# AdaLN block on one core: another order of the first superblock (silu, LayerNorm in pieces, q's first product, h's low part on VectorE)

## Chip, cores, metric

One core of a Trainium2 chip. The metric is the device time of one launch in microseconds. Time before: median 930.48 us of 3 runs (928.63 to 931.09).

Engines are named as the profile names them: PE is TensorE's matmul, PEld its weight load, DVE is VectorE, ACT ScalarE, POOL GpSimd, SP SyncE. PSUM has 8 banks of 512 fp32 per partition.

## What is computed

x has 4096 tokens of 256 features. Six vectors come from a small modulation product; the block is a gated attention with softmax over features and tokens (linear attention), and a mixture of 8 experts, 2 per token.

```python
mod = (silu(c) @ wmod).reshape(6, 256)          # sa, ca, ga, sb, cb, gb
ga, gb = (2 * (g >= 0) - 1) * maximum(abs(g), 0.25)
h = layernorm(x) * (1 + ca) + sa
q, k, v = split(h @ w_qkv)                      # 16 heads of 64
q = softmax(q * 64**-0.5, axis=-1)              # over the 64 features of a head
k = softmax(k, axis=-2)                         # over the 4096 tokens
context = einsum('bhnd,bhne->bhde', q, k)
out = einsum('bhde,bhnd->bhne', context, v)
x = x + ga * (merge(out) @ w_out + b_out)
h = layernorm(x) * (1 + cb) + sb
x = x + gb * moe(h)                             # top 2 of 8 experts, gelu, 1024 hidden
```

## The kernel before

The program is written engine by engine, each engine's instructions in a fixed order by hand; engines wait for each other on counting semaphores (`s_...`), and `after(eng, s, n)` is such a wait for n > 0. There is no planner: what stands behind a waiting instruction on its engine waits too.

**Tiling.** The 32 tiles of 128 tokens form 8 superblocks (SBN) of 4 tiles (ST). The k loop has 64 steps n = (superblock s, head pair j), 8 per superblock. The products with w_qkv are made exact by splitting both sides: w into `wqk_hi` (a rounded copy by ScalarE) and `wqk_lo` (the rest, `w_low` on DVE), h into `h_q[..., 0]` (high part, ScalarE, `h_hi`) and `h_q[..., 1]` (low part, GpSimd, `h_lo`, from the full h in `h_all`). A product is three terms per 128 features: 6 matmuls of 512 columns.

**Stages of a superblock.** DVE makes LayerNorm's statistics (`layer_norm`, lines 834 to 847: one bn_stats per tile, one bn_aggr per tile, then 12 small linked operations for the inverse root, each waiting for the one before). ScalarE normalises (`norm_x`, L632), PE transposes x (`x_T`, L1209), ScalarE and GpSimd make h_hi, h_all and h_lo (L620, L622, L498). Then PE makes q per tile (`q_mm`, L1227, both halves of 512 columns), DVE subtracts the maximum (`q_a`, L856 and L857), ScalarE takes the exponential (`q_e`, L638), DVE sums (`q_b`, L863 and L864), and GpSimd normalises (`q_norm`, L504).

**A step of the k loop** on PE: the k product of head pair j (`k_mm`, L1266), the four transposes of the k of the step before (`k_T`, L1275), the context product of three steps before (`c_mm`, L1285), in j = 3 the x transposes of superblock s + 2, and one half of a q product of superblock s + 1 (L1227). On DVE (lines 926 to 948): `acc` adds a finished context product (L924), `k_m` the running maximum (L916, L917), then q_a in even steps or q_b in odd ones; after step 7 `layer_norm((4, 5, 6, 7))`, after step 15 the gates (L943 to L948). On ScalarE: `k_e` (the exponential of k, L649, and the rescaling factor, L651), `k_ev` (L643), `norm_x` in j = 0 and 1, `h_hi` in j = 3, `q_e` in even steps.

**What stands before the loop.** SP issues the loads in this order (L407 to L422): c, b1, x of superblock 0, wmod's first third, w_q, w_k, x of superblock 1, the rest of wmod, four small ones, x of superblocks 2 to 7, w_out. DVE: `layer_norm((0,))`, silu, memset of ctx_acc, w_low(0), the first modulation's copies, w_low(1 to 3), the second modulation's copies, `layer_norm((1,))`, q_a(0, 0), q_a(0, 1), the gating weights (L899 to L903), q_b and q_a of the other tiles, `layer_norm((2, 3))`, q_b(0, 3). PE: first modulation (L1198), x_T(0), second modulation and gate rows (L1198, L1240), q_mm(0, 0), q_mm(0, 1), x_T(1), gating products (L1250, L1254), q_mm(0, 2), q_mm(0, 3), loop. ScalarE: silu's exponential, norm_x(0), w's high parts for q (L659), h_hi(0), those for k (L665), norm_x(1), q_e(0, 0), q_e(0, 1), h_hi(1), q_e(0, 2), q_e(0, 3), loop. `LN_OF` says which LayerNorm call a superblock waits for.

After the loop the context is folded with w_out and w_v, the residual, the second LayerNorm and the routing are done, and the experts run in hardware loops; that part (from about 350 us on) is not touched.

Of the kernel before, what the change touches and what calls it, by code (L numbers as in the profile page):

```python
# [82 lines left out]
def adaln_block(nc, x, w_qkv, w_out, b_out, Wg, bg, W1, b1, W2, b2, cvec, wmod, out):  # L83
    ctx = ExitStack()
    with ctx:
# [176 lines left out]
        s_hhi = sem("s_hhi")  # L262
        s_hlo = sem("s_hlo")
        s_kt = sem("s_kt")
        s_nm = sem("s_nm")
# [74 lines left out]
        DMA2 = 32  # L340
        CONSTS = 7
        IOTAS = 5


        KT, TR, CX = 4, 6, 7
        LN_OF = (0, 1, 2, 2, 3, 3, 3, 3)
        KN = SBN * J
# [10 lines left out]
        def xt_bank(s, c):  # L358

            return (TR, CX)[c] if s == 1 else c  # L360

# [39 lines left out]
        def _(sp):  # L401
# [10 lines left out]
            wqk_t = w_qkv[:, 0:2 * HD].rearrange("(c p) n -> p c n", p=P)  # L412
            sp.dma_start(wqk_raw[:, :, 0:HD], wqk_t[:, :, 0:HD]).then_inc(s_wq, 16)
            sp.dma_start(wqk_raw[:, :, HD:2 * HD], wqk_t[:, :, HD:2 * HD]).then_inc(s_wk, 16)
            sp.dma_start(x_all[:, ST:2 * ST, :], x_t[:, ST:2 * ST, :]).then_inc(s_x[1], 16)
            sp.dma_start(wmod_sb[:, :, 2 * D:6 * D], wmod_t[:, :, 2 * D:6 * D]).then_inc(s_wmod[1], 16)
            sp.dma_start(bo_bc[:, :], b_out.partition_broadcast(P)).then_inc(s_small, 16)
            sp.dma_start(bg_bc[:, :], bg.partition_broadcast(P)).then_inc(s_small, 16)
            sp.dma_start(wg_raw[:, :, :], Wg.rearrange("(c p) e -> p c e", p=P)).then_inc(s_small, 16)
            for s in range(2, SBN):  # L420
                sp.dma_start(x_all[:, s * ST:(s + 1) * ST, :], x_t[:, s * ST:(s + 1) * ST, :]).then_inc(s_x[s], 16)
# [56 lines left out]
        def _(pool):  # L478
# [14 lines left out]
                      allow_small_or_imprecise_dtypes=True).then_inc(s_const, 1)  # L493

            def h_lo(s, c):

                pool.wait_ge(s_hhi, s * C + (c + 1))
                pool.tensor_tensor(h_q[:, s % HB, 1, c, :], h_all[:, c, s * STOK:(s + 1) * STOK], h_q[:, s % HB, 0, c, :].bitcast(F32), ALU.subtract).then_inc(s_hlo, 1)  # L498
# [17 lines left out]
            for s in range(-1, SBN - 1):  # L516
                if s == -1:
                    for c in range(C):
                        h_lo(0, c)
                q_norm(s + 1, 0)  # L520
                if s + 2 < SBN:
                    for c in range(C):
                        h_lo(s + 2, c)
                for i in range(1, ST):
                    q_norm(s + 1, i)
                if s >= 1:
                    add_bias(s - 1)
# [82 lines left out]
        def _(act):  # L610
            act.sem_inc(s_gelu, FOUR)

            def h_hi(s, c):

                act.wait_ge(s_xt, s * C + (c + 1))
                if c == 0 and s >= HB:
                    act.wait_ge(s_kt, (s - HB + 1) * J)
                    act.wait_ge(s_hlo, (s - HB + 1) * C)
                bank = xt_bank(s, c)
                act.activation(h_q[:, s % HB, 0, c, :], ps[:, bank, :], ACT.Identity, bias=modc[:, 0, c:c + 1],  # L620
                               scale=modc[:, 1, c:c + 1])
                act.activation(h_all[:, c, s * STOK:(s + 1) * STOK], ps[:, bank, :], ACT.Identity, bias=modc[:, 0, c:c + 1],  # L622
                               scale=modc[:, 1, c:c + 1]).then_inc(s_hhi, 1)
# [30 lines left out]
            act.wait_ge(s_cTc, 1)  # L654
            act.activation(silu_t[:, :], silu_c[:, :], ACT.Exp, scale=-1.0).then_inc(s_silu_e, 1)
            norm_x(0)
            act.wait_ge(s_wq, 16)
            for c in range(C):
                act.activation(wqk_hi[:, c, 0:HD], wqk_raw[:, c, 0:HD], ACT.Copy).then_inc(s_whqk, 1)  # L659
            act.wait_ge(s_modr, 1)  # L660
            for c in range(C):
                h_hi(0, c)
            act.wait_ge(s_wk, 16)
            for c in range(C):
                act.activation(wqk_hi[:, c, HD:2 * HD], wqk_raw[:, c, HD:2 * HD], ACT.Copy).then_inc(s_whqk, 1)  # L665
            norm_x(1)
            q_e(0, 0)
            q_e(0, 1)
            for c in range(C):
                h_hi(1, c)  # L670
            q_e(0, 2)
            q_e(0, 3)

            for n in range(KN):
# [10 lines left out]
                if j % 2 == 0:  # L685
                    if j and s + 1 < SBN:
                        q_e(s + 1, j // 2 - 1)
                    elif not j and s:
                        q_e(s, ST - 1)
# [128 lines left out]
        def _(dve):  # L818
# [14 lines left out]

            def layer_norm(sbs):

                r = slice(sbs[0] * ST, (sbs[-1] + 1) * ST)
                for s in sbs:
                    dve.wait_ge(s_x[s], 16)
                    for t in range(s * ST, (s + 1) * ST):
                        last = dve.bn_stats(ln_s[:, t, :], x_all[:, t, :])  # L840
                link(last)
                for t in range(r.start, r.stop):
# [23 lines left out]
            def w_low(n):  # L866

                dve.wait_ge(s_whqk, n + 1)
                col = slice((n // C) * HD, (n // C + 1) * HD)
                dve.tensor_tensor(wqk_lo[:, n % C, col], wqk_raw[:, n % C, col], wqk_hi[:, n % C, col].bitcast(F32), ALU.subtract).then_inc(s_wlqk, 1)  # L870

            layer_norm((0,))
            dve.wait_ge(s_cT, 1)
# [6 lines left out]
            dve.tensor_copy(silu_b[:, :, :], bc(silu_c[:, :], 2, [P, C, P])).then_inc(s_silu, 1)  # L880
            dve.memset(ctx_acc[:, :, :], 0.0)
            link(dve.memset(k_new[:, 1, :], BIG))
            w_low(0)
            dve.wait_ge(s_mod, 1)
            link(dve.tensor_copy(modc[:, 0:2, :].rearrange("p k c -> p (k c)"), ps[:, MA, 0:2 * C]))
            dve.tensor_scalar(modc[:, 1, :], modc[:, 1, :], 1.0, None, ALU.add).then_inc(s_modr, 1)
            w_low(1)
            w_low(2)
            w_low(3)
            dve.wait_ge(s_mod, 2)  # L890
            link(dve.tensor_copy(modc[:, 2:4, :].rearrange("p k c -> p (k c)"), ps[:, MB, 0:2 * C]))
            link(dve.tensor_scalar(modc[:, 3, :], modc[:, 3, :], 1.0, None, ALU.add))
            dve.tensor_copy(shift_b[:, :, :], bc(modc[:, 2, :], 2, [P, C, P]))
            dve.tensor_copy(gate_raw[:, :, :].rearrange("p k d -> p (k d)"), ps[:, MG, :]).then_inc(s_modr, 1)
            layer_norm((1,))
            q_a(0, 0)
            q_a(0, 1)
            dve.wait_ge(s_small, 48)
            dve.tensor_tensor(wg_mod[:, :, :], wg_raw[:, :, :], bc(modc[:, 3, :], 2, [P, C, E]), ALU.mult).then_inc(s_wgm, 1)  # L899
            dve.wait_ge(s_bgp, 1)  # L900
            dve.tensor_tensor(bg_bc[:, :], bg_bc[:, :], ps[:, MB, 0:E], ALU.add)
            dve.wait_ge(s_wgm, 1)
            dve.tensor_tensor(wg_mod[:, :, :], wg_mod[:, :, :], bc(ps[:, MB, E:2 * E], 1, [P, C, E]), ALU.subtract).then_inc(s_bgr, 1)  # L903
            q_b(0, 0)
            q_a(0, 2)
            q_b(0, 1)
            q_a(0, 3)
            q_b(0, 2)
            layer_norm((2, 3))
            q_b(0, 3)  # L910

# [14 lines left out]
            for n in range(KN):  # L926
                s, j = divmod(n, J)
                for m in products(n - 1):
                    acc(m)
                k_m(n)  # L930
                s_, i = (s + 1, j // 2 - 1) if j >= 2 else (s, ST - 1)
                if 0 < s_ < SBN:
                    if j % 2:
                        q_b(s_, i)
                    else:
                        q_a(s_, i)
                if s == SBN - 1 and j == 1:
                    dve.wait_ge(s_xt, SBN * C)
                    dve.memset(ctx_n[:, :, :], 0.0).then_inc(s_zero, 1)
                if s == 0 and j == 7:  # L940
                    layer_norm((4, 5, 6, 7))
                if s == 1 and j == 7:
# [240 lines left out]
        def _(pe):  # L1183
# [28 lines left out]
            def q_mm(s, i, halves=(0, 1)):  # L1212

                n = s * ST + i
                if 0 in halves:
                    if i == 0:
                        pe.wait_ge(s_hlo, s * C + C)
                    if i == 2 and 1 <= s < SBN - 1:
                        pe.wait_ge(s_hhi, (s + 2) * C)
                    after(pe, s_qs, n - 1)  # L1220
# [13 lines left out]
            pe.wait_ge(s_cTc, 1)  # L1234
            x_T(0)
            pe.wait_ge(s_wmod[1], 16)
            modulation(MB, (3, 4))
# [4 lines left out]
            last.then_inc(s_mod, 1)  # L1242
            pe.wait_ge(s_wlqk, 2)
            q_mm(0, 0)
            q_mm(0, 1)
            pe.wait_ge(s_modr, 2)
            x_T(1)
            pe.wait_ge(s_small, 48)
# [6 lines left out]
            last.then_inc(s_bgp, 1)  # L1255
            q_mm(0, 2)
            q_mm(0, 3)
            pe.wait_ge(s_wlqk, 4)
            pe.wait_ge(s_bgr, 1)
# [210 lines left out]
```

## Time and profile before

| | us |
|---|---|
| median of 3 runs | 930.48 |
| profiled execution | 930.57 |
| its span | 928.8 |
| PE busy | 827.7 (89%) |
| DVE busy | 569.8 (61%) |
| ACT busy | 498.5 (54%) |
| POOL busy | 335.7 (36%) |
| mean granted TensorE clock | 0.949 of full |

The span runs from the first to the last recorded instruction; the execution's own time has 1.7 us around it. Busy shares are means over stages with different limits. In the page's picture of 40 slices (23 us each), PE's digits begin with 5 8 4 9 7: the two low ones (slices 0 and 2) are the start and the entry to the k loop. Matmul ends are modelled, and consecutive matmuls overlap in the records: six of 512 columns take 1.39 us of the chain though each row shows 0.39.

### The profile page before, as it was taken

Reading aid. Unit: us, or ns where it says so; the run is one execution under the profiler, and the core shown is the slowest. Engines: PE = TensorE matmul, PEld = TensorE weight load, DVE = VectorE, ACT = ScalarE, POOL = GpSimd, SP = SyncE. Lnnn points to the kernel's source line nnn. Section 1 sums busy time; section 2 is a strip of 40 time slices with the busy share of each in tenths; the row PEclk is TensorE's granted clock in tenths of the full one; section 3 lists DMA queues with packets and bytes.
Section 4 is the critical chain, followed back from the end, with each engine's and each line's share of the span. In section 5 each row is a group of like instructions: output and inputs, shape, how many; then the busy total and the mean of one; then the engine's idle time right before and its main releaser. Section 6 shows DMA issues by size and latency. Waiting matters only on the chain.

```text
span 928.8 us, 17546 instructions
## 1 busy us (share of the span) xinstructions
PE 827.7 (89%) x5836; PEld 771.0 (83%) x5837; DVE 569.8 (61%) x1257; ACT 498.5 (54%) x978; POOL 335.7 (36%) x304
## 2 busy tenths in 40 slices
PE   5849789999999879985499999999999999999994
PEld 4638678888888767974399999899999999999994
DVE  4667787777777642579455644656546565665552
ACT  4325446456554341369475755657566565755552
POOL 1223133333332230300124545445445554444442
PEclk9879899999999998995599999999999999999998
DMA  8300000000000003234534252424325252222222
GB/s 292 100 0 1 1 1 1 1 1 1 1 1 1 25 25 122 92 128 136 160 71 91 46 134 44 130 46 112 58 46 136 46 130 42 45 46 45 41 47 28
DMA packets 45212, 57.50 MB, mean 62 GB/s; under 512 B 7794, under 2 KB 39220, under 8 KB 45044
## 3 DMA queue, kind: packets, MB, share of 16 engines
q0 software_dynamic: 14400, 20.24, 13.7%
q1 hardware_dynamic: 30772, 36.76, 11.8%
q8 instruction: 21, 0.34, 0.2%
q14 instruction: 19, 0.16, 0.1%
HBM read 38.24 MB, written 18.75 MB: 61 GB/s over the span
## 4 chain that ended last, share of the span: by engine, by line
PE 72%; DVE 14%; issue 6%; ACT 4%; DMA 2%; POOL 1%; DVEq 0%; SPq 0%; ACTq 0%; POOLq 0%
PE ps L1433 22%; PE ps L1421 18%; PE ps L1266 7%; PE ps L1227 7%; PE ps L1285 5%; PE ps L1335 3%; PE ps L1404 2%; PE ps L1275 2%; DVE q_max L856 2%; ACT at_lo L736 2%; DVE w_lo L1170 2%; DMA wmod_sb<-in_L_wmod 1%; DVE k_blk L916 1%; PE ps L1355 1%; DVE w_lo L1167 1%
## 5 line engine op out<-in xcount | busy, mean ns | idle before, releaser
L791 ACT ACTIVATE hid<-ps,b_col 128x256 f32<-128x256 f32 x296 | 122.3, 464 | 114.4 <-PE ps L1421 98.5
L1433 PE MATMUL ps<-w_hi,hid_hi 128*128 128x256 f32 x592 | 170.9, 289 | 10.0 <-DVE hid_lo L1150 10.0
L1150 DVE TENSOR_TENSOR hid_lo<-hid,hid_hi 128x512 fp32r<-128x512 f32 x148 | 100.6, 691 | 119.5 <-ACT hid_hi L799 118.6
L1421 PE MATMUL ps<-xT_hi,w_hi 128*128 128x256 f32 x592 | 168.5, 285 | 2.2 <-DVE xT_lo L1127 2.2
L1421 PE MATMUL ps<-xT_hi,w_lo 128*128 128x256 f32 x592 | 168.2, 284 | 0.0
L1421 PE MATMUL ps<-xT_lo,w_hi 128*128 128x256 f32 x592 | 168.1, 284 | 0.0
L1433 PE MATMUL ps<-w_hi,hid_lo 128*128 128x256 f32 x592 | 166.5, 281 | 0.0
L1433 PE MATMUL ps<-w_lo,hid_hi 128*128 128x256 f32 x592 | 166.4, 281 | 0.0
L580 POOL DMA_INDIRECT out<-y,y_id x74 | 126.5, 1709 | 51.8 <-DVE y L1159 34.6
L504 POOL TENSOR_TENSOR q_n<-q_exp,q_rec 128x1024 f32<-128x1024 f32 x32 | 61.0, 1906 | 214.1 <-DVE q_rec L864 214.1
L1433 PEld LDWEIGHTS ps<-w_hi,hid_hi 128*128 128x128 f32 x592 | 111.5, 188 | 12.2 <-DVE hid_lo L1150 12.2
L1421 PEld LDWEIGHTS ps<-xT_hi,w_hi 128*128 128x128 f32 x592 | 113.7, 192 | 2.6 <-issue 2.6
L1421 PEld LDWEIGHTS ps<-xT_lo,w_hi 128*128 128x128 f32 x592 | 113.8, 192 | 0.0
L1421 PEld LDWEIGHTS ps<-xT_hi,w_lo 128*128 128x128 f32 x592 | 113.7, 192 | 0.0
L1433 PEld LDWEIGHTS ps<-w_lo,hid_hi 128*128 128x128 f32 x592 | 111.9, 189 | 0.0
L1433 PEld LDWEIGHTS ps<-w_hi,hid_lo 128*128 128x128 f32 x592 | 111.4, 188 | 0.0
L649 ACT ACTIVATE k_exp<-ps,k_new 128x512 f32<-128x512 f32 x64 | 44.0, 687 | 122.8 <-DVE k_new L917 122.8
L799 ACT ACTIVATE hid_hi<-hid 128x512 fp32r<-128x512 f32 x148 | 93.5, 632 | 10.9 <-issue 5.2
L1227 PE MATMUL ps<-wqk_hi,h_q 128*128 128x512 f32 x256 | 97.9, 427 | 0.0
L568 POOL DMA_INDIRECT listed<-xrows,gid x76 | 80.5, 1059 | 43.6 <-POOL gid L564 32.1
L916 DVE TENSOR_REDUCE k_blk<-ps 128x1 f32<-128x512 f32 x64 | 44.1, 689 | 68.5 <-PE ps L1266 68.5
L1285 PE MATMUL ps<-q_n,k_tok 128*128 128x128 f32 x512 | 70.1, 281 | 17.4 <-DVE ctx_acc L924 16.9
(194 smaller groups left out, 1511.2 us busy)
## 6 DMA issues: line engine op xcount, KB each, us to landing
w_raw<-in_L_ffn_W SPq DMA_DIRECT2D x16, 1024.0 KB
x_all<-in_L_attn_x SPq DMA_DIRECT2D x8, 512.0 KB, 10.6
out<-x_all SPq DMA_DIRECT2D x8, 512.0 KB, 3.0
xrows<-x_all SPq DMA_DIRECT2D x8, 512.0 KB, 3.0
wqk_raw<-in_L_attn_w_qkv SPq DMA_DIRECT2D x2, 1024.0 KB, 8.8
listed<-xrows,gid POOLq DMA_INDIRECT x76
out<-y,y_id POOLq DMA_INDIRECT x74
wmod_sb<-in_L_wmod SPq DMA_DIRECT2D x1, 1024.0 KB, 12.9
```

Source lines behind the costliest of these rows:

```text
L504: pool.tensor_tensor(q_n[:, s % 2, i, :].rearrange("p (h d) -> p h d", d=DH), q_exp[:, i % 2, :].rearrange("p (h d) -> p h d", d=DH), bc(q ...
L568: pool.indirect_dma_start(listed[:, i, :], None, xrows[:, :], bass.IndirectOffsetOnAxis(ap=gid[:, i:i + 1], axis=0)).then_inc(s_rows, 16)
L580: pool.indirect_dma_start(out[:, :], bass.IndirectOffsetOnAxis(ap=y_id[:, i:i + 1], axis=0), y[:, i, :], None, compute_op=ALU.add).then_in ...
L791: ins = act.activation(hid[:, m, :], ps[:, k, (m % 2) * BT:(m % 2 + 1) * BT], ACT.Gelu_apprx_tanh, bias=b1_col[:, bass.ds(e, 1), m])
L799: act.activation(hid_hi[:, m, :], hid[:, m, :], ACT.Copy).then_inc(s_hidhi, 1)
L916: link(dve.tensor_reduce(k_blk[:, j:j + 1], ps[:, KT + n % 2, :], AX, ALU.max, negate=True))
L1150: dve.tensor_tensor(hid_lo[:, m, :], hid[:, m, :], hid_hi[:, m, :].bitcast(F32), ALU.subtract).then_inc(s_hid, 1)
L1227: last = pe.matmul(ps[:, b + half, :], a, w, start=st, stop=sp_)
L1266: last = pe.matmul(ps[:, KT + n % 2, :], w, a, start=st, stop=sp_)
L1285: last = pe.matmul(ps[:, CX, 0:P], k_tok[:, n % KR, t, :], q_n[:, s % 2, t, j * P:(j + 1) * P], start=t == 0, stop=t == ST - 1)
L1421: last = pe.matmul(ps[:, k, (m % 2) * BT:(m % 2 + 1) * BT], w, a, start=st, stop=sp_)
L1433: last = pe.matmul(ps[:, Y0 + i, 0:D], a, w, start=m == 0 and st, stop=m == M - 1 and sp_)
```

## The change

- **Start.** silu's operations come ahead of LayerNorm 0 on DVE; the memset of ctx_acc moves to GpSimd. `layer_norm` is split into `ln_stats(tiles)` and `ln_finish(superblocks)`.
- **Transfers.** x of superblocks 1 and 2 is loaded ahead of w_k.
- **h of superblock 0.** ScalarE makes only the high part; DVE makes the full h and the low part itself (`h_0`), GpSimd's h_lo(0) goes. The transposed x of superblock 0 lies in banks 2 and 3.
- **w of q.** It is split in halves of 512 columns on ScalarE (`w_high`) and DVE (`w_low(0..3)`); w_k keeps its two full ones (`w_low(4)`, `w_low(5)`).
- **q's first product** is written out: the terms with h's high part first for each half, those with the low part last. It and q_mm(0, 1) come ahead of the second modulation.
- **Second modulation** is read later by DVE, behind LayerNorm 1 and 2, q_a(0, 1), q_b(0, 0), w_low(4) and w_low(5); the gate rows are copied by ScalarE (semaphore `s_modg`), which x_T(1) waits for.
- **q's last tile.** q_b(0, 2), q_a(0, 3), q_b(0, 3) and q_e(0, 3) move into steps 0 and 1 of the loop.
- **LayerNorm.** Superblocks 1 and 2 together before the loop; statistics of 3 tiles in each of steps 1, 3, 5 (8 tiles in all), the finish of superblocks 3 and 4 in step 7; statistics of 2 tiles in each odd step from 9 to 19, the finish of 5 to 7 in step 21.

The diff without its context lines, with 8 columns of indentation cut and the two new semaphores left out:

```diff
-CONSTS = 7
+CONSTS = 8
...
-LN_OF = (0, 1, 2, 2, 3, 3, 3, 3)
+LN_OF = (0, 1, 1, 2, 2, 3, 3, 3)
...
-    return (TR, CX)[c] if s == 1 else c
+    return (TR, CX)[c] if s == 1 else 2 + c if s == 0 else c
...
+    for s in (1, 2):
+        sp.dma_start(x_all[:, s * ST:(s + 1) * ST, :], x_t[:, s * ST:(s + 1) * ST, :]).then_inc(s_x[s], 16)
...
-    sp.dma_start(x_all[:, ST:2 * ST, :], x_t[:, ST:2 * ST, :]).then_inc(s_x[1], 16)
...
-    for s in range(2, SBN):
+    for s in range(3, SBN):
...
+    pool.memset(ctx_acc[:, :, :], 0.0).then_inc(s_const, 1)
...
-        if s == -1:
-            for c in range(C):
-                h_lo(0, c)
...
-            act.wait_ge(s_hlo, (s - HB + 1) * C)
+            after(act, s_hlo, (s - HB) * C)
...
-        act.activation(h_q[:, s % HB, 0, c, :], ps[:, bank, :], ACT.Identity, bias=modc[:, 0, c:c + 1],
-                       scale=modc[:, 1, c:c + 1])
+        hi = act.activation(h_q[:, s % HB, 0, c, :], ps[:, bank, :], ACT.Identity, bias=modc[:, 0, c:c + 1],
+                            scale=modc[:, 1, c:c + 1])
+        if s == 0:
+            hi.then_inc(s_hhi, 1)
+            return
...
+    def w_high(half, c):
+        col = slice(half * 512, (half + 1) * 512)
+        act.activation(wqk_hi[:, c, col], wqk_raw[:, c, col], ACT.Copy).then_inc(s_whqk, 1)
...
-    for c in range(C):
-        act.activation(wqk_hi[:, c, 0:HD], wqk_raw[:, c, 0:HD], ACT.Copy).then_inc(s_whqk, 1)
+    w_high(0, 0)
+    w_high(0, 1)
...
+    w_high(1, 0)
+    w_high(1, 1)
...
+    q_e(0, 0)
...
-    q_e(0, 0)
...
+    act.wait_ge(s_mod, 2)
+    act.activation(gate_raw[:, :, :].rearrange("p k d -> p (k d)"), ps[:, MG, :], ACT.Copy).then_inc(s_modg, 1)
...
-    q_e(0, 3)
...
-            elif not j and s:
+            elif not j:
...
-    def layer_norm(sbs):
+    def ln_stats(tiles):
+        for t in tiles:
+            if t % ST == 0:
+                dve.wait_ge(s_x[t // ST], 16)
+            last = dve.bn_stats(ln_s[:, t, :], x_all[:, t, :])
+        return last
+    def ln_finish(sbs):
...
-        for s in sbs:
-            dve.wait_ge(s_x[s], 16)
-            for t in range(s * ST, (s + 1) * ST):
-                last = dve.bn_stats(ln_s[:, t, :], x_all[:, t, :])
-        link(last)
...
-        col = slice((n // C) * HD, (n // C + 1) * HD)
+        col = slice((n // C) * 512, (n // C + 1) * 512) if n < 2 * C else slice(HD, 2 * HD)
...
-    layer_norm((0,))
+    def h_0(c):
+        dve.wait_ge(s_hhi, c + 1)
+        link(dve.tensor_scalar(h_all[:, c, 0:STOK], ps[:, xt_bank(0, c), :], modc[:, 1, c:c + 1], modc[:, 0, c:c + 1], ALU.mult, ALU.add))
+        dve.tensor_tensor(h_q[:, 0, 1, c, :], h_all[:, c, 0:STOK], h_q[:, 0, 0, c, :].bitcast(F32), ALU.subtract).then_inc(s_hlo0, 1)
...
-    dve.memset(ctx_acc[:, :, :], 0.0)
+    link(ln_stats(range(ST)))
+    ln_finish((0,))
...
+    w_low(1)
...
-    w_low(1)
+    dve.wait_ge(s_modr, 1)
+    h_0(0)
+    h_0(1)
...
+    q_a(0, 0)
+    link(ln_stats(range(ST, 3 * ST)))
+    ln_finish((1, 2))
+    q_a(0, 1)
+    q_b(0, 0)
+    w_low(4)
+    w_low(5)
...
-    dve.tensor_copy(shift_b[:, :, :], bc(modc[:, 2, :], 2, [P, C, P]))
-    dve.tensor_copy(gate_raw[:, :, :].rearrange("p k d -> p (k d)"), ps[:, MG, :]).then_inc(s_modr, 1)
-    layer_norm((1,))
-    q_a(0, 0)
-    q_a(0, 1)
+    dve.tensor_copy(shift_b[:, :, :], bc(modc[:, 2, :], 2, [P, C, P])).then_inc(s_modr, 1)
...
+    q_b(0, 1)
+    q_a(0, 2)
...
-    q_b(0, 0)
-    q_a(0, 2)
-    q_b(0, 1)
-    q_a(0, 3)
-    q_b(0, 2)
-    layer_norm((2, 3))
-    q_b(0, 3)
+    dve.wait_ge(s_const, CONSTS)
...
+        if n == 0:
+            q_b(0, 2)
...
-        if 0 < s_ < SBN:
+        if s_ < SBN:
...
+        if s == 0 and j in (1, 3, 5):
+            t = 3 * ST + 3 * (j // 2)
+            link(ln_stats(range(t, min(t + 3, 5 * ST))))
...
-            layer_norm((4, 5, 6, 7))
+            ln_finish((3, 4))
+        if j % 2 and J < n < 2 * J + 4:
+            t = 5 * ST + 2 * (n // 2 - J // 2)
+            link(ln_stats(range(t, t + 2)))
+        if s == 2 and j == 5:
+            ln_finish((5, 6, 7))
...
-                pe.wait_ge(s_hlo, s * C + C)
+                after(pe, s_hlo, s * C)
...
+    steps = [(half, 0, c, low) for half in range(2) for c in range(C) for low in range(2)] + \
+            [(half, 1, c, 0) for half in range(2) for c in range(C)]
+    for half, h_low, c, w_low in steps:
+        if h_low:
+            pe.wait_ge(s_hlo0, c + 1)
+        else:
+            pe.wait_ge(s_hhi, c + 1)
+            pe.wait_ge(s_wlqk, half * C + c + 1)
+        w = (wqk_hi, wqk_lo)[w_low]
+        last = pe.matmul(ps[:, half, :], h_q[:, 0, h_low, c, 0:P], w[:, c, half * 512:(half + 1) * 512],
+                         start=(h_low, c, w_low) == (0, 0, 0), stop=(h_low, c) == (1, C - 1))
+    last.then_inc(s_q, 1)
+    q_mm(0, 1)
...
-    pe.wait_ge(s_wlqk, 2)
-    q_mm(0, 0)
-    q_mm(0, 1)
+    q_mm(0, 2)
+    pe.wait_ge(s_modg, 1)
+    x_T(1)
...
-    x_T(1)
...
-    q_mm(0, 2)
...
-    pe.wait_ge(s_wlqk, 4)
+    pe.wait_ge(s_wlqk, 6)
```

## Rows read from the trace of the kernel before

**Rows 1.** The chain of waits, in order of time: start us, duration us, what.
```profile
4.58 12.87 DMA wmod_sb<-in_L_wmod
...
17.49 3.57 PE ps L1198 x16
...
59.35 1.43 DVE k_new L917
...
74.94 0.44 PE ps L1275 x4
...
75.37 0.89 PE ps L1285 x8
...
76.27 1.39 PE ps L1227 x6
...
77.66 1.39 PE ps L1266 x6
```

**Rows 2.** Timeline of PE: start, duration, instruction, in brackets idle time before it.
```profile
44.20 0.63 PE L1266 MATMUL ps<-h_q,wqk_hi 128*128 128x512 f32 x2
...
61.54 1.11 PE L1275 MATMUL ps<-ident,k_exp 128*128 128x128 f32 x4 [12.98 <-ACT k_exp L649]
...
71.12 1.04 PE L1209 MATMUL ps<-ident,xn 128*128 128x128 f32 x8
...
99.13 2.04 PE L1285 MATMUL ps<-q_n,k_tok 128*128 128x128 f32 x8 [7.30 <-DVE ctx_acc L924]
...
138.11 1.13 PE L1285 MATMUL ps<-q_n,k_tok 128*128 128x128 f32 x8 [2.89 <-DVE ctx_acc L924]
```

**Rows 3.** Stretches: length, busy us per engine, then PEclk, DMA share, GB/s.
```profile
36.00:41.30 5.30, 5.30 (x14) 4.21 (x14) 1.63 (x4) 2.79 (x5) 3.27 (x3) 0.50 0.01 3
...
48.50:61.50 13.00, 0.06 (x1) 0.00 (x0) 12.35 (x39) 1.75 (x3) 3.80 (x2) 0.62 0.00 0
```

**Rows 4.** Timeline of DVE, start to step 15.
```profile
5.51 1.41 DVE L840 BATCH_NORM_STATS2 ln_s<-x_all 128x6 f32<-128x256 f32 x4 [5.37 <-DMA x_all<-in_L_attn_x]
...
13.37 1.23 DVE L870 TENSOR_TENSOR wqk_lo<-wqk_raw,wqk_hi 128x1024 fp32r<-128x1024 f32 x1 [1.00 <-ACT wqk_hi L659]
...
30.16 1.22 DVE L856 TENSOR_REDUCE q_max<-ps 128x16 f32<-128x1024 f32 x1
...
32.55 1.22 DVE L856 TENSOR_REDUCE q_max<-ps 128x16 f32<-128x1024 f32 x1
...
51.41 2.65 DVE L840 BATCH_NORM_STATS2 ln_s<-x_all 128x6 f32<-128x256 f32 x8
...
57.27 1.21 DVE L863 TENSOR_REDUCE q_sum<-q_exp 128x16 f32<-128x1024 f32 x1
...
83.20 0.69 DVE L916 TENSOR_REDUCE k_blk<-ps 128x1 f32<-128x512 f32 x1 [1.64 <-PE ps L1266]
...
89.54 5.26 DVE L840 BATCH_NORM_STATS2 ln_s<-x_all 128x6 f32<-128x256 f32 x16
...
98.64 0.34 DVE L924 SCALAR_TENSOR_TENSOR ctx_acc<-ctx_acc,k_alpha,ps 128x128 f32<-128x128 f32 x1
...
132.93 0.36 DVE L943 TENSOR_SCALAR wvT<-wvT 128x512 f32<-128x512 f32 x1
...
133.21 2.12 DVE L944 TENSOR_SCALAR wvT<-wvT 128x512 f32<-128x512 f32 x1
...
137.63 0.34 DVE L924 SCALAR_TENSOR_TENSOR ctx_acc<-ctx_acc,k_alpha,ps 128x128 f32<-128x128 f32 x1
```

**Rows 5.** Timelines of ACT and POOL.
```profile
10.26 2.06 ACT L632 ACTIVATE xn<-x_all,ln_b,ln_r 128x256 f32<-128x256 f32 x4
...
15.96 0.78 ACT L620 ACTIVATE h_q<-ps,modc 128x512 fp32r<-128x512 f32 x1 [1.75 <-PE ps L1209]
...
17.49 2.60 POOL L498 TENSOR_TENSOR h_q<-h_all,h_q 128x512 fp32r<-128x512 f32 x2 [14.94 <-ACT h_all L622]
...
133.10 1.95 POOL L504 TENSOR_TENSOR q_n<-q_exp,q_rec 128x1024 f32<-128x1024 f32 x1 [6.23 <-DVE q_rec L864]
```

More of the change, by code:

```diff
@@ L263, in adaln_block @@
         s_hlo = sem("s_hlo")
+        s_hlo0 = sem("s_hlo0")
+        s_modg = sem("s_modg")
         s_kt = sem("s_kt")
```

## The prediction

> **What bounds the kernel now.** I read the chain of waits first, then the order of work on TensorE with its idle times, then the stretches with the granted clock, and last the VectorE rows inside the idle stretches. The chain [rows 1] starts at a transfer: the second part of wmod lands at 17.45 us. After that it is short stretches of VectorE and long ones of TensorE. In the k loop one step costs TensorE four pieces: q half 1.39, k product 1.39, four transposes 0.44, context product 0.89, together 4.11 us. The reader is to see that this is the price of a step when nothing is late, and that eight steps and one set of x transposes (0.87; 1.04 in rows 2 with its drain) make 33.8 us for a superblock.
>
> The order on TensorE [rows 2] shows where it is more. The first k product starts at 43.98 (the row's first record, 44.20, is the same product). Then TensorE stands 12.98 us before the transposes of step 0, 7.30 us before the context product of step 7, and 2.89 us before that of step 15. The x transposes of superblock 2, my marker below, start at 71.12. In an undisturbed loop they would come 11.9 us after its start (three k products and three q halves of 1.39, two sets of transposes of 0.44, and in step 3 a k product, transposes and the first context product, 1.39 + 0.44 + 0.89), not 27.1 us. The stretches [rows 3] add that the clock had fallen: 0.62 on average in the idle one, and 0.50 in 36.0 to 41.3, where one tile's q product (12 matmuls) took 5.3 us against 2 x 1.39 in rows 1. Behind the stops of 12.98 and 7.30 us TensorE also runs its first groups at the low level (1.2 GHz). Behind 7.30 us that is a context product of 2.04 us against 1.13 behind the stop of 2.89 us, and the same 0.9 on the q half after it, 1.8 us; behind 12.98 us the transposes and one q half and a bit, 2.0 us. After 2.89 us the clock had not fallen.
>
> What VectorE does in those stops [rows 4]: before step 0 it runs q's last tiles and LayerNorm of superblocks 2 and 3 (51.41 to 57.27, 5.86 us) while k's product has long been ready; at step 7 LayerNorm of superblocks 4 to 7 (89.54 to 98.64, 9.10 us); at step 15 the gates (132.93 to 137.63, 4.70 us). So a block of X us on VectorE in an odd step stops TensorE for X - 1.8 us: 9.10 gives 7.30, 4.70 gives 2.89. I use this twice-measured allowance for the new pieces.
>
> **The change, part by part.**
>
> *Start, to the first q product.* silu goes ahead of LayerNorm 0. LayerNorm waits for x until 5.51 [rows 4], silu's inputs are there before, so silu is done near 5.4 (its chain is 1.4 us by the same instructions' spacing) and LayerNorm 0 ends at 5.51 + 1.41 + 3.0 = 9.9, as before. The finish is 3.0 because that of two superblocks is 5.86 - 2.65 = 3.2. The first modulation can then run from about 7 (it needs its part of wmod), 3.6 us [rows 1], and ends at 10.6. It hides behind LayerNorm, and the change gets nothing from it at once: norm_x takes 2.06 [rows 5], the eight x transposes at the low level twice the 0.87 of full rate, so 12.0 to 13.8. VectorE does two half-width w_low (half of 1.23, 0.65 each) after ScalarE's half-width copies and only then reads the modulation: scale and shift are ready at 14.3. ScalarE's h: two of 0.78, without the two h_all copies between; ready 15.1 and 15.8. VectorE's h_0: a scaled copy of 512 from PSUM and a subtraction, 0.65 to 0.7 each, 1.35 per half: ends 16.5 and 17.85. Two more w_low: 19.1. TensorE does the high half of the first product at 15.2 to 16.9, then waits for w_low(2) at 18.5 and needs 8 more matmuls at 0.43 (5.3 us for 12, rows 3): q's first product is complete at 22.0. Before, it stood behind the second modulation and the gates, which start at 17.49 and take 3.57 [rows 1] and as much again, so near 27.5: this edit does deliver some 5 us there.
>
> *To the k loop; VectorE is the path here.* q_a costs 2.39 (30.16 to 32.55, rows 4), q_b a sum of 1.21 and a reciprocal, 1.42. From 22.0: q_a(0,0) to 24.4; stats of 8 tiles 2.65 to 27.05; finish 3.2 to 30.2; q_a(0,1) to 32.6; q_b(0,0) to 34.05; w_low(4), w_low(5), 1.23 each, to 36.4; the second modulation's copies 0.7 to 37.1; wg_mod 0.2; q_b(0,1) 1.4; q_a(0,2) 2.4; the last gating step 0.3: sum 41.5. That has no wait in it. TensorE beside it: q_mm(0,1) 22 to 27, second modulation and gates 3.6 + 3.5 at the low level or half of it, q_mm(0,2) done by 33.7. All of that is hidden. The moved DMAs: x of superblock 2 goes ahead of wk and wmod's second part, 0.5 MB. The six transfers up to wmod's second part are 4.5 MB and land between 1.9 and 17.45 [rows 1], 0.29 MB per us, so this is 1.7 us: wmod's part lands at about 19 instead of 17.45, needed at 26 to 27; wk at about 16, needed at 16.7. Cost nothing. POOL's new memset of ctx_acc stands in its idle first 17 us; VectorE's 0.9 us for it goes.
>
> *The wait that this order adds.* GpSimd normalises q (1.9 us) as soon as q_b(0,0) is done, and makes h_lo of superblock 1 (2 x 1.3 us, rows 5) as soon as ScalarE has h. Now VectorE's w_low(4), w_low(5), the modulation copies and wg_mod fall in just these microseconds. Rows: k_new at 59.35 took 1.43 us instead of 0.16 and ended when GpSimd's q_n did [rows 1]; a tensor_scalar at 133.21 took 2.12 [rows 4] instead of 0.43 and ended with the q_n of 133.10 [rows 5]; q_max, q_exp and bn_stats beside GpSimd work kept their times. So: q_n's 1.9 us goes in somewhere before the modulation copies (38.3), one h_lo (1.3) before shift_b or wg_mod (39.9 to 41.2), and the rest follows: gating step done between 43.8 and 45.4. What is queued behind it is TensorE: its last gating matmuls (some 1.5 to 1.9 us at the low level, as TensorE has been idle since 35), then q_mm(0,3), 5.1 us at that level or some 4 if the clock rises inside, then the loop. That gives a loop start T0 between 45.2 and 47.4; without any such wait, 42 to 44.2. I take 45.8, nearer the rows.
>
> The Trainium skill, page "SBUF — State Buffer", section "Who interferes with whom", has the rule: a VectorE instruction with two SBUF inputs, or a copy or tensor_scalar in a two-port mode, and a GpSimd instruction that reads SBUF exclude each other, and tensor_reduce never does. By this rule, which speaks against the change, every finish of LayerNorm right behind a q_b is caught; without it the sum would be some 6 us better. By this rule, the trace agrees: 1.43, 2.12 and their GpSimd partners.
>
> *In the first steps of the loop.* q_b(0,2), q_a(0,3), q_b(0,3) are now inside. VectorE: k_m(0) from T0 + 1.4 to 2.3, q_b to 3.7, q_a to 6.1, k_m(1) to 6.95; ScalarE has q_e(0,3) ahead of k_e(1), ready 7.9, then k_ev(0) 8.6; TensorE's transposes of step 1 wait for it from 7.4 to 8.7, those of step 2 from 11.9 to 12.45, and the x transposes of superblock 2 start at T0 + 13.8 = 59.6. Before: 71.12. The 12.98 us stop and its 2.0 of clock become 1.8 us of small waits. Gain so far 11.5.
>
> *LayerNorm in pieces.* Three tiles of bn_stats are 3/8 of 2.65 = 1.0 us in steps 1, 3, 5; two are 0.66 in steps 9 to 19. An odd step has 1.6 us free on VectorE before the next k_m (the 1.8 allowance): no cost. The finishes are the cost. Finish of superblocks 3 and 4 in step 7: 3.15 us, but q_n has just started when it gets to its first small operation, so X = 2.0 + 2.45 = 4.5, stop 2.7 (without that wait 1.35). Step 15: the gates, with 0.66 of stats ahead, X = 5.1, stop 3.3 (before 2.89). Finish of 5 to 7 in step 21: X = 4.55, stop 2.75 (1.7). Sum 8.75. Before: 7.30 + 1.8 + 2.89 = 12.0. Gain 3.25. None of the three is long enough to lower the clock, by the 2.89 us stop.
>
> Everything behind the loop is released by its end and shifts with it. Sum: 11.5 + 3.25 = 14.75. The profiled execution took 930.57 us (span 928.84 and 1.73 around it), the median is 930.48, so 930.57 - 14.75 = 915.8 us.
>
> **Rivals.**
> 1. *The waits between VectorE and GpSimd hardly land* (instructions slip in between). T0 43, and the finishes cost 1.35, 2.9 and 1.7: gain 71.1 - 56.8 + 12.0 - 5.95 = 20.3, 910.3 us. For it: a tensor_scalar at 132.93, started just ahead of q_n, took only 0.36 [rows 4]; who starts first is not held up. Against: the rows above.
> 2. *VectorE's backlog at the loop start is larger*: with two q tiles and a piece of LayerNorm inside steps 0 to 3, each waiting for ScalarE in turn, two of the first steps lose 1.8 us more (the allowance, missed twice: 3.6) and the clock falls once (1.9, the mean of the two above). 915.8 + 5.5 = 921.3. For it: VectorE is busy 12.35 of 13 us in 48.5 to 61.5 [rows 3], and part of that work is only moved.
> 3. *Slower: the clock stays low.* If the first superblock's loop starts at 1.2 GHz and the many short waits hold it there, each step costs TensorE 4.11 us more. It decides from 3.6 steps on (14.75 / 4.11); for the whole superblock the price is 33.8 us, 949.6. Against: after a stop of 12.98 us, with small stops to follow, the clock was back by 71.12, where eight transposes take 1.04 us [rows 2].
> 4. *The gain is eaten*: LayerNorm's work is the same total, and if each piece stopped TensorE by its length (pieces 3 x 1.0 + 6 x 0.66 and finishes), 7 us would return and T0 at 47.4 takes 1.6 more; 924 us with the small waits, and with a longer one 929. Against: idle VectorE time of 1.64 us before 83.20 [rows 4].
>
> **How the numbers follow.** Forecast 0.52, rival 1 0.22, rival 2 0.14, rival 3 0.04, rival 4 0.08 (a quarter of it within 0.3% of no change). The forecast's own range is 913 to 919 (T0 from 45.2 to 47.4, the finishes by 1.35 either way). With rival 1 and most of rival 2: 909.5 to 921.5. 0.3% is 2.8 us, about what a measurement here can tell from no change. Faster by more: 0.94; within: 0.02; slower: 0.04.
>
> **What would show it.** Right: q's first product done near 22, one w_low or shift_b of 2 us or more near 35 to 41, first k product at 45 to 47.5, x transposes of superblock 2 at 58.5 to 61, no TensorE stop over 4 us in the loop, stops of 2 to 3.5 at steps 7, 15 and 21. Wrong: a first k product before 44, or a stop over 5 us in steps 0 to 3, or the low clock after step 4.

## The result, and the profile after

The changed kernel takes 922.12 us (median of 4 runs, 919.13 to 924.75) against 929.87 us for the kernel before: ratio 0.992, 95% interval 0.9902 to 0.9938. Forecast were 915.8 us and a range of 909.5 to 921.5. The direction was right; of the 14.75 us forecast, 7.75 came by the medians. The profiled run is the slowest of the four, 924.75 us (span 922.9), 5.8 us below the profiled run of before. The order of the four times is that of their mean granted clock: 919.13 us with 0.955 of full, 921.5 with 0.953, 922.75 with 0.952 and 924.75 with 0.948. What is read from the profiled run below is so the dear end; the median is 2.6 us cheaper.

The page after, for the shares and the clock:

```profile
span 922.9 us, 17565 instructions
PE 832.6 (90%) x5836; PEld 773.6 (84%) x5837; DVE 575.2 (62%) x1261; ACT 498.2 (54%) x979; POOL 337.0 (37%) x303
PE   5798988999999879984599999999999999999994
PEclk9799989999999999985599999999999999999998
```

PE's slice 2, which was 4 before, is now 9: the large stop ahead of step 0 is gone. But the busy sum of PE went up by 5 us (832.6 against 827.7) with the same number of matmuls. PE did no more work; it did more of it at the lower clock.

PE's timeline after (start, duration, instruction, idle time before it), the answer to [rows 2]:

```profile
35.02 1.92 PE L1243 MATMUL ps<-ident,xn 128*128 128x128 f32 x8 [2.25 <-ACT wvT L682]
41.27 1.02 PE L1296 MATMUL ps<-wg_raw,shift_b 128*128 128x8 f32 x4 [4.33 <-DVE shift_b L925]
42.99 0.77 PE L1261 MATMUL ps<-wqk_hi,h_q 128*128 128x512 f32 x1
...
48.26 0.88 PE L1311 MATMUL ps<-h_q,wqk_hi 128*128 128x512 f32 x2
...
62.34 1.04 PE L1243 MATMUL ps<-ident,xn 128*128 128x128 f32 x8
...
85.69 1.45 PE L1330 MATMUL ps<-q_n,k_tok 128*128 128x128 f32 x8 [2.64 <-DVE ctx_acc L948]
...
124.78 2.05 PE L1330 MATMUL ps<-q_n,k_tok 128*128 128x128 f32 x8 [3.18 <-DVE ctx_acc L948]
...
157.56 1.63 PE L1330 MATMUL ps<-q_n,k_tok 128*128 128x128 f32 x8 [2.81 <-DVE ctx_acc L948]
```

Here the whole account can be read. The x transposes of superblock 2, the marker, come at 62.34 instead of 71.12: 8.8 us gained. The three stops are 2.64, 3.18 and 2.81 us, forecast 2.7, 3.3 and 2.75. The loop's first product starts at 48.26, later than before (44.20; the row at 43.98, which the forecast read as this product, is the last matmul of q's, L1227) and 2.5 us later than forecast.

The chain of waits behind the stops (start, duration, what):

```profile
85.69 1.45 PE ps L1330 x8
87.14 2.56 PE ps L1261 x6
89.70 1.47 PE ps L1311 x6
91.17 0.44 PE ps L1320 x4
...
124.78 2.05 PE ps L1330 x8
126.82 2.56 PE ps L1261 x6
129.38 2.06 PE ps L1311 x6
...
157.56 1.63 PE ps L1330 x8
159.19 2.48 PE ps L1261 x6
```

At full clock the context product behind a stop takes 1.13 us [rows 2] and six matmuls 1.39 [rows 1]. Behind the stop of step 7 they take 0.32, 1.17 and 0.08 us more, together 1.6; behind that of step 15, 0.92, 1.17 and 0.67, together 2.8; behind that of step 21, 0.50 and 1.09, together 1.6. These 5.9 us were in no term of the sum. They turn the gain of 3.25 us that was forecast behind the marker into a loss: (2.64 + 3.18 + 2.81 + 5.9) against 12.0 before, 2.5 us. 8.8 - 2.5 is 6.3, and the profiled runs differ by 5.8. Most of the half microsecond between them is a wait for GpSimd's q_n near 320 us, 0.76 us long and 0.42 before.

DVE's timeline after, between q_b(0, 0) and the loop, with POOL's beside it:

```profile
34.73 4.00 DVE L886 TENSOR_TENSOR wqk_lo<-wqk_raw,wqk_hi 128x1024 fp32r<-128x1024 f32 x2
38.65 0.15 DVE L923 COPY modc<-ps 128x4 f32<-128x4 f32 x1
38.83 1.04 DVE L924 TENSOR_SCALAR modc<-modc 128x2 f32<-128x2 f32 x1
39.90 1.31 DVE L925 COPY shift_b<-modc 128x256 f32<-128x256 f32 x1
```
```profile
34.90 2.75 POOL L509 TENSOR_TENSOR q_n<-q_exp,q_rec 128x1024 f32<-128x1024 f32 x1 [31.44 <-DVE q_rec L880]
37.65 3.41 POOL L503 TENSOR_TENSOR h_q<-h_all,h_q 128x512 fp32r<-128x512 f32 x2
```

The two w_low take 4.00 us instead of 2 x 1.23, the addition on 2 columns at L924 1.04 us instead of 0.17, shift_b 1.31 instead of 0.29; and GpSimd is held up too, 2.75 instead of 1.9 and 3.41 instead of 2.6 [rows 5]. The forecast had the second modulation read at 38.3 and shift_b ready between 39.9 and 41.2; it is ready at 41.2.

### The profile page after: what moved, and what is told of

It is laid out like the page before. It is cut to its first block, busy times and chain, and to the rows that moved or that the text cites. A ratio compares the mean times of both kernels' runs of the same rounds, so it can differ in the third digit from the quotient of the medians.

```text
span 922.9 us, 17565 instructions
## 1 busy us (share of the span) xinstructions
PE 832.6 (90%) x5836; PEld 773.6 (84%) x5837; DVE 575.2 (62%) x1261; ACT 498.2 (54%) x979; POOL 337.0 (37%) x303
## 4 chain that ended last, share of the span: by engine, by line
PE 72%; DVE 15%; issue 6%; ACT 5%; POOL 1%; DVEq 0%; DMA 0%; ACTq 0%; POOLq 0%
PE ps L1478 22%; PE ps L1466 18%; PE ps L1311 7%; PE ps L1261 7%; PE ps L1330 5%; PE ps L1380 3%; PE ps L1449 2%; ACT at_lo L749 2%; DVE w_lo L1204 2%; DVE q_max L872 2%; PE ps L1320 2%; DVE k_blk L940 1%; PE ps L1400 1%; DVE w_lo L1201 1%; DVE q_sum L879 1%
```

## Experiments

All medians are of 4 to 17 runs; ratios are to the kernel before on the same chip. The kernels ran on several chips, and the median of the kernel before differed between them by 1.1 us (928.94 to 930.02), so differences of that size between medians say nothing. Each trace is one execution, and the clock in it need not be that of the median run. The theory, formed from the two traces: the change's start gives the loop nothing by itself; the stops in the loop cost their length plus a stretch of low clock; both come from small VectorE work put beside GpSimd's.

**The later LayerNorms in one block (e1).**

```diff
-        # the pieces in steps 1 to 21
+        if s == 0 and j == 7:
+            link(ln_stats(range(3 * ST, TILES)))
+            ln_finish((3, 4, 5, 6, 7))
```

> The changed kernel with LayerNorm of superblocks 3 to 7 as one block after step 7 (statistics of 20 tiles and one finish), no pieces. Theory (stops of 2.6 to 3.2 us cost as much again by the low clock behind them, so pieces bring nothing): one stop of 8.8 us plus 1.8 of clock at step 7 in place of 2.64 + 1.56 there and 2.81 + 1.6 at step 21, and the gates' stop back to 2.9 with less of clock; sum 13.5 against 14.9, so the same or 0 to 2 us faster than the changed kernel, 920 to 922. Rival (pieces are worth what was forecast, the loss lies in the start): 3 to 5 us slower than the changed kernel, 925 to 927.

Measured: 922.73 us, ratio 0.9932 (0.9912 to 0.9953), the same as the changed kernel and 0.7 above what the theory gave. Its one large stop is 8.90 us; the gates' stop of 2.88 us had the clock at 0.50 in the 5 us behind it. Cutting LayerNorm into these pieces brought nothing.

**The pieces alone (e2)**, in the kernel before.

```diff
+        if s == 0 and j in (3, 5):      # statistics of tiles 16 to 19
+        if s == 0 and j == 7: ln_finish((4,))
+        # statistics of 2 tiles in odd steps 9 to 19; in step 21:
+        ln_finish((5, 6, 7))
-        if s == 0 and j == 7: layer_norm((4, 5, 6, 7))
```

> The kernel before with only LayerNorm of superblocks 4 to 7 in pieces (4 finished in step 7, 5 to 7 in step 21). Theory (low clock behind every stop of about 3 us): takes away 7.3 + 1.8, adds 2.3 + 1.6 and 2.8 + 1.6 and makes the gates' stop 0.3 longer: within 1.5 us of before, 928.5 to 931. Rival: 3 to 4 us faster, 926.

Measured: 928.03 us, ratio 0.9986 (0.9974 to 0.9997). That is half a microsecond below what was expected, and from the other side the same: about 1 us of 929. Its trace already spoke against the theory's "every stop": behind the stops of 2.59 and 3.17 us the clock was 0.66 and 0.69, behind that of 2.78 us it was 1.00.

**The loop's part alone (e8)**: before, with LayerNorm 1 and 2 together, x of superblock 2 early, q's last tile in the loop, the pieces; none of the new start order.

```diff
-layer_norm((1,))
+layer_norm((1, 2))
-q_a(0, 3); q_b(0, 2); layer_norm((2, 3)); q_b(0, 3)
+# q_b(0, 2), q_a(0, 3), q_b(0, 3) in steps 0 and 1
```

> The kernel before with only the loop's part of the change: LayerNorm of 1 and 2 together (x of superblock 2 loaded early), q's last tile in the loop's first steps, the later LayerNorms in pieces. silu's order, the split of h, the half-width w and the order of q's first product are as before. Theory (the new start order brings the loop no earlier, since it puts w_low and the modulation's copies beside GpSimd's work and leaves TensorE idle ahead of its last product): loop starts at 45.7 instead of 48.3, 919 to 921, as fast as the changed kernel or up to 3 us faster. Rival (the start order is worth the 5 us by which q's first product comes earlier): 926 to 928.

Measured: 922.78 us, ratio 0.9918 (0.9902 to 0.9934), as fast as the changed kernel and 1.8 us above the expected 921. The loop starts at 47.4 and not at the expected 45.7: here too TensorE is behind with q's last product. With the new start order it began between 46.95 and 48.26 in six profiled kernels whose start is the same (the changed one, e1, e4, e6, e11, e12), so the two orders can't be told apart. All of the gain is then this part's; silu first, h's low part on VectorE, half-width w and the early first product, as they stand in the change, bring the loop no earlier.

**w_low(4) and w_low(5) early (e3).**

```diff
 w_low(2)
 w_low(3)
+w_low(4)
+w_low(5)
 q_a(0, 0)
```

> The changed kernel with w_low(4) and w_low(5) ahead of q_a(0, 0), in VectorE's idle 3.3 us at 19.3, instead of behind q_b(0, 0) where the two took 4.0 us beside GpSimd's q_n. Theory (VectorE is the path to the loop, and half of the 4.0 us is the wait for GpSimd): the second modulation's shift_b ready 2 to 3.5 us earlier (the modulation's small copies now meet q_n themselves), k loop starts 2 to 3.5 us earlier, 919 to 920. Rival (TensorE at the low clock, not VectorE, sets the loop's start): under 1 us.

Measured: 919.03 us, ratio 0.9892 (0.9867 to 0.9916). In the profiled run the four take 3.56 us in idle time, shift_b is ready at 36.8 instead of 41.2, and the loop starts at 43.2 instead of 48.3. That is 5.0 us in the trace, more than expected, and 3.1 in the median. The runs lie between 914.61 and 920.53, and the profiled one is the fastest; its q product was done 0.6 us sooner, partly at full clock. The rival, under 1 us, falls. But TensorE is on the same path: its last product waits for shift_b and the loop for it, as e7 shows.

**q's last product early (e7).**

```diff
 q_mm(0, 2)
+q_mm(0, 3)
 pe.wait_ge(s_modg, 1)
```

> The changed kernel with q's product of tile 3 ahead of x_T(1) and the gating products. Theory (at the loop's start TensorE works 5.3 us on it at the low clock while VectorE is done at 45.2): the loop starts at 45.2 to 46 instead of 48.3, 919 to 920; the first steps are at the low clock instead, which may give 1 to 2 us back. Rival (VectorE sets the start): no change, 922.

Measured: 918.75 us, ratio 0.9876 (0.9857 to 0.9895). The loop starts at 45.4, as VectorE's gating step ends; its first product runs at the low clock. The marker moves from 62.34 to 60.57. So VectorE up to shift_b and TensorE's 5.3 us behind it set the start together.

**Finishes and gates ahead of q_b (e4).**

```diff
 k_m(n)
+if s == 0 and j == 7: ln_finish((3, 4))
+if s == 2 and j == 5: ln_finish((5, 6, 7))
+if s == 1 and j == 7: ...               # the gates
 q_b(s_, i)                              # in even steps q_a
-# the same three behind it
```

> The changed kernel with both finishes of LayerNorm and the gates ahead of q_a or q_b of their step, so that GpSimd's q_n isn't running beside them. Theory (each waited 1.3 to 1.5 us for q_n, and the clock falls for stops near 3 us): blocks of 3.1, 3.1 and 3.5 us instead of 4.3, 4.9 and 4.5, stops of 1.3 to 1.7 each, and no low clock behind at least two of them: 4 to 8 us faster than the changed kernel, 914 to 918. Rival (the clock falls behind any stop, or q_b's delay is as long): under 2 us faster.

Measured: 915.08 us, ratio 0.984 (0.9817 to 0.9862), 7.0 us better than the changed kernel, with the same instructions. The chain after and the timeline of this kernel show the finish in step 7:

```profile
80.84 0.51 DVE ln_a L859 x8
81.35 0.02 issue
81.37 1.49 DVE ln_v L861
...
85.11 0.04 DVE ln_b L863
```
```profile
78.13 0.64 DVE L859 BATCH_NORM_AGGREGATE ln_a<-ln_s 128x2 f32<-128x6 f32 x8
78.80 0.17 DVE L861 TENSOR_SCALAR ln_v<-ln_a 128x8 f32<-128x8 f32 x1
81.23 0.17 DVE L863 SCALAR_TENSOR_TENSOR ln_b<-ln_a,ln_r 128x8 f32<-128x8 f32 x1
```

With q_n running, one operation on 8 columns takes 1.49 us; without, 0.17. The block is 3.2 us instead of 4.3. Its stops on PE:

```profile
83.14 1.13 PE L1330 MATMUL ps<-q_n,k_tok 128*128 128x128 f32 x8 [1.31 <-DVE ctx_acc L948]
...
119.77 1.13 PE L1330 MATMUL ps<-q_n,k_tok 128*128 128x128 f32 x8 [1.97 <-DVE ctx_acc L948]
...
150.13 1.13 PE L1330 MATMUL ps<-q_n,k_tok 128*128 128x128 f32 x8 [1.55 <-DVE ctx_acc L948]
```

The stops are 3.8 us shorter in sum (4.83 for 8.63). The low clock behind them costs 1.6 us here, 5.9 in the changed kernel's trace. With the marker 1.2 us earlier (61.11, the same instructions) this covers the 9.0 us between the two profiled runs. Of the 7.0 us between the medians the shorter stops give 3.8. In the 5 us behind each stop it was 1.00, 0.66 and 1.00 of full here, and 0.66, 0.50 and 0.66 in the changed kernel. The context product alone doesn't tell it: the one at 119.77 still takes 1.13 us, and the q half behind it 2.19 instead of 1.39:

```profile
119.77 1.13 PE ps L1330 x8
120.90 2.19 PE ps L1261 x6
123.09 2.16 PE ps L1311 x6
```

So my "no low clock behind at least two of them" holds, with one of three lowered behind a stop of only 1.97 us. Nor is this the same in every execution: of the five runs two took 913.1 us with a mean clock of 0.960 and three 915.1 to 915.7 with 0.956 to 0.957.

**Both (e5):** e3 and e4 in one kernel, no further edit.

> Both edits that helped at once: w_low(4) and w_low(5) early, finishes and gates ahead of q_b. Theory (the two act in different places and add up): 3.1 + 7.0 us below the changed kernel's 922.1, 912 us. Rival (the earlier loop start only moves a later wait): 915, as the second edit alone.

Measured: 911.02 us, ratio 0.978 (0.9763 to 0.9797), 1 us below what was expected. They add up (by the ratios, even to somewhat more).

**The parts spread (e6).**

```diff
+n in (1, 3, 9, 11, 17): link(ln_stats(range(t, t + 4)))
+n == 5:  ln_finish((3, 4), range(0, 6))
+n == 7:  ln_finish((3, 4), range(6, 14))
+n == 13: first three operations of the gates
+n == 15: last three
+n == 19, 21, 23: ln_finish((5, 6, 7)) in three parts
```

> The changed kernel with the finishes and the gates cut into parts of at most 1.6 us, one part in each odd step, ahead of q_b (statistics of 4 tiles in steps 1, 3, 9, 11, 17; finish of 3 and 4 in 5 and 7; gates in 13 and 15; finish of 5 to 7 in 19, 21, 23). Theory (an odd step hides 1.6 to 1.8 us on VectorE; stops and the low clock behind them are all that was lost): no stop at all at steps 7, 15, 21, TensorE at full clock from step 2 on: 8.6 us of stops and some 4 to 6 of clock less, 908 to 911. Rival (a stop only comes back elsewhere, as the parts eat the idle time of even steps): 914 to 916.

Measured: 909.0 us, ratio 0.977 (0.9757 to 0.9783), the five runs between 908.69 and 909.05. Between 60 and 300 us, changed kernel and then this one (length; busy us and count of PE, PEld, DVE, ACT, POOL; clock; DMA share; GB/s):

```profile
60.00:300.00 240.00, 227.24 (x1289) 192.52 (x1288) 185.34 (x329) 123.76 (x227) 76.09 (x43) 0.97 0.00 1
```
```profile
60.00:300.00 240.00, 233.08 (x1352) 198.35 (x1353) 192.59 (x342) 129.59 (x237) 78.09 (x44) 0.99 0.00 1
```

63 more matmul records go through in the same time. No stop is left at steps 7, 15 and 21; 0.19 and 0.62 us remain elsewhere, as before.

**The old start with the spread loop (e10):** e8 with the parts of e6.

> The kernel before with its own start order and the spread loop: e8 with the finishes and gates in parts as in e6. Theory (the new start order, silu first, h's low part on VectorE, half-width w and q's first product early, is worth nothing for the loop's start): 909 to 910, as e6. Rival (it is worth something that the stops hid in e8): 912 or more.

Measured: 908.95 us, ratio 0.9775 (0.9753 to 0.9798), the same as e6. With a clean loop behind it the new start order, as it stands in the change, is again worth nothing.

**A stop made on purpose (e11, e12)** in step 15 of e6:

```diff
+for extra in range(10):                 # e12: 5
+    last = dve.bn_stats(ln_s[:, 8 + extra, :], x_all[:, 8 + extra, :])
```

> The spread kernel (e6) with 10 needless bn_stats (3.3 us) in step 15: one stop of about 3 us at an otherwise clean loop. Theory (a stop of this length costs its own length and, in some runs and not in others, 1.5 to 3 us of low clock behind it): 909.0 + 3 + 0 to 3, median near 913.5, and the runs lie 2 us or more apart where those of e6 lay within 0.4. Rival (the stop costs its length only): 912.0, runs within 0.6 us.

> The spread kernel (e6) with 5 needless bn_stats (1.6 us) in step 15: a stop of about 1.3 us. Theory (stops under 2 us leave the clock): 910.3, runs within 0.6 us. Rival (any stop may lower the clock): 911 to 912.5 and runs 1.5 us or more apart.

Measured: e11 911.58 us (0.9818, 0.9793 to 0.9843), e12 909.3 us (0.979, 0.9765 to 0.9816). The profiled runs, e11 and then e12:

```profile
120.48 1.80 PE L1355 MATMUL ps<-q_n,k_tok 128*128 128x128 f32 x8 [2.96 <-DVE ctx_acc L966]
```
```profile
119.80 1.13 PE L1355 MATMUL ps<-q_n,k_tok 128*128 128x128 f32 x8 [1.34 <-DVE ctx_acc L966]
```

The stop of 2.96 us has the clock at 0.66 in the 5 us behind it, the one of 1.34 at 1.00. But my median was 2 us too high: 911.58 lies nearer the rival's 912.0, while the spread of 2.8 us speaks for the theory. e11's runs lie in two groups, 911.2 to 911.6 us (mean clock 0.958 and 0.959) and 914.0 (0.955 and 0.957); so do e12's, 908.5 to 909.3 (0.960) and 911.5 to 911.6 (0.956), which the theory denied for a short stop. The added stop need not be the place: all these kernels have another stop of 2.40 us near 300 us, and in 290 to 300 us, ahead of and behind it, the two profiled runs (e6, then e12) read:

```profile
290.00:300.00 10.00, 7.61 (x40) 6.41 (x39) 4.38 (x8) 2.41 (x4) 1.91 (x1) 0.83 0.00 0
```
```profile
290.00:300.00 10.00, 7.60 (x49) 6.56 (x49) 5.94 (x11) 3.77 (x7) 1.91 (x1) 1.00 0.00 0
```

In e12's profiled run, and in e11's, the clock does not fall there; in e6's it does. Whether it is the added stop that does this, by shifting the later one, is not shown: these are single executions. The spread of the runs can't be put down to the added stop alone.

**All of it (e9):** e6 with e3 and e7.

> The spread kernel (e6) with w_low early (e3) and q's product of tile 3 early (e7). Theory (start and loop add up; with both edits at the start VectorE is done at 40.7 and TensorE has nothing left before the loop, so the loop starts at 41 instead of 48.3, partly at the low clock): 909.0 - 5 to 7, 902 to 904. Rival (one of the two start edits makes the other idle): 905 to 906.

Measured: 903.82 us (901.13 to 904.05), ratio 0.971 (0.9686 to 0.9735), as expected. The loop starts at 41.3. It is the best version here, 25 us below the kernel before and 18 below the changed one. The 5 us over e6 were won in the new start order; whether the old one, with its own products moved in the same way, would do as well was not tried.

## Why the forecast was off, step by step

- *Start, to q's first product:* right. Forecast 22.0; VectorE's q_a began at 22.59. LayerNorm 0 ended at 9.8 (9.9), scale and shift were read at 13.8 to 14.1 (14.3).
- *To the k loop:* mechanism right, size off. The waits between VectorE and GpSimd came as listed, at the upper end of their bounds: gating step done at 45.2 (forecast 43.8 to 45.4). Then TensorE ran q's last product wholly at the low clock, 42.99 to 48.26. The terms were right and added up wrongly: shift_b at 41.2, gating matmuls 1.9 and the product 5.1 at the low level give 48.2, not the 47.4 written as the upper end, and 45.8 was a choice below both. The term was 2.5 us too small in this run, 1.1 to 2.5 over the six profiled runs with this start.
- *The first steps of the loop:* right, T0 + 14.1 for T0 + 13.8, with waits of 1.25 and 0.27 us.
- *LayerNorm in pieces:* the stops are right within 0.12 us each; the allowance of 1.8 us per odd step held. **The step that failed is the last one: "None of the three is long enough to lower the clock, by the 2.89 us stop".** One row of a stop without low clock behind it was taken for a rule, though the same trace has a row against it, a stop of 2.41 us near the loop's end:

```profile
316.51 1.13 PE L1285 MATMUL ps<-q_n,k_tok 128*128 128x128 f32 x8 [2.41 <-DVE ctx_acc L924]
```
```profile
138.11:143.11 5.00, 5.00 (x33) 4.43 (x33) 4.26 (x8) 3.52 (x7) 0.00 (x0) 1.00 0.00 0
316.51:321.51 5.00, 5.00 (x24) 4.42 (x25) 1.94 (x4) 1.40 (x3) 0.00 (x0) 0.66 0.00 0
```

These are the 5 us behind the stops of 2.89 and 2.41 us in the kernel before: clock 1.00 and 0.66. In the changed kernel the clock fell behind all three stops, 5.9 us in the profiled run; the median run is 2.6 us faster at a higher mean clock. Over all profiled runs of this study (clock in the 5 us behind the stop): of the 18 stops of 2.59 to 3.18 us at steps 7, 15 and 21, 11 had the clock below full behind them (0.50 to 0.70) and 7 had it at 1.00, among these 3.17 us (e3, e7) as well as 2.63 (e8); both of 1.97 and 1.98 (e4, e5) had it at 0.66; the five of 1.30 to 1.57 (e4, e5, e12) at 1.00; those of 7.3 us and more were all followed by low clock. The stop of 2.40 or 2.41 us near the loop's end, which all fourteen kernels have, had 0.66 behind it in eleven and 1.00 in three (e1, e11, e12).
- With these errors mended (2.5 for the loop's start, 0.3 for its first steps, 5.9 for the clock) the sum is 930.57 - (14.75 - 2.5 - 0.3 - 5.9) = 924.5; the profiled run took 924.75. The median, 922.12, is 6.3 us above the forecast.
- *Rivals:* rival 1 (no waits between VectorE and GpSimd) is refuted by the rows at 34.73 to 39.90. Rival 2's price (two missed allowances) did not come, but its half about the clock did, at other places. Rival 4 came nearest in size with another mechanism: the pieces did give back what they took, not by their length but by the clock behind each finish (e1, e2). Rival 3 did not happen.
- The page of the Trainium skill cited in the forecast ("SBUF — State Buffer", section "Who interferes with whom") held: tiny operations with SBUF operands waited for q_n, tensor_reduce and bn_stats did not, and taking the finish out of q_n's way (e4) took 1.1 us off the block in step 7 and 1.2 to 1.3 us off each of the three stops.

What stays open: why the clock falls behind one stop of 2.4 to 3.2 us and not behind another of the same length or longer, and not in every execution of one kernel. When a stop falls is a rival to its length that is left untested: no run here controlled it.

## What to carry to other kernels

When TensorE is the bound, price a stop by its length and by what the first matmuls behind it take in the trace, and give a stop of 2 to 3 us both values; one sample of either is no rule. Small linked operations on VectorE belong ahead of the instruction that releases GpSimd, not behind it: the same instructions in another place were worth 7 us, with the clock that came back. Cut a block to what a step really hides (1.6 us here); pieces above that, each with its own stop, were worth nothing against one large block.

## What the runs showed that I had not expected

- GpSimd loses as well when both want SBUF: its q_n took 2.75 us instead of 1.90 beside two w_low, and two h_lo 3.41 instead of 2.6.
- An earlier intermediate result (q's first product at 22 instead of about 27 us) moved the loop's start not at all: e8 and e10, without it, are as fast as the changed kernel and e6.
- The five runs of e6 lie within 0.4 us and those of e10 within 1.3; the four of the changed kernel, with three more stops of about 3 us, span 5.6 us.
